# A selective-scan phase on one core: the position term by TensorE, the residual by TensorE and ScalarE, and paired input products

## The reference, cut to what matters

```python
x = x + L1_conv(ln_c(x), pos, W_in, conv_w, ...)      # ln_c: norm over the 64 channels of a pixel

xw = windows(x)                  # [b*nh*nw, 64, 8, 8]
xw = xw + pos                    # one position table for every window
seq = xw.reshape(b, 64, 64).transpose(0, 2, 1)        # 64 steps of 64 channels
x, z = split(seq @ W_in)         # 128 and 128 channels
x = silu(causal_conv(x, conv_w, 4 taps, by channel) + conv_b)
dt, B, C = split(x @ W_xproj)    # 4, 16, 16
dt = softplus(dt @ W_dt + b_dt)
h  = exp(dt * A) * h + (dt * x) * B      # 128 channels x 16 states, 64 steps, one after the other
y  = sum_n(h * C) + x * Dp
out = (y * silu(z)) @ W_out
```

## Time and profile before

| | |
|---|---|
| median of three runs | 8556.24 us |
| the profiled execution | 8588.41 us, span 8586.6 us |
| VectorE busy | 6791.2 us, 79% of the span |
| TensorE busy | 6282.9 us, 73% |
| GpSimd busy | 5185.6 us, 60% |
| ScalarE busy | 4293.2 us, 50% |
| DMA | 1253.45 MB, mean 146 GB/s |
| TensorE's granted clock, mean | 0.82 of full |

### The profile page before, as it was taken

The page is one execution under the profiler, slowest core; times in us unless marked ns, Lnnn a source line. Parts: engine busy times, 40 slices in busy tenths (PEclk is TensorE's granted clock), DMA queues, the critical chain, the costliest instruction groups (busy, mean ns, idle before and its releaser), DMA issues. The chain is left out here.

```text
span 8586.6 us, 102988 instructions
## 1 busy us (share of the span) xinstructions
PE 6282.9 (73%) x30668; PEld 2512.8 (29%) x30668; DVE 6791.2 (79%) x7924; ACT 4293.2 (50%) x5876; POOL 5185.6 (60%) x1723
## 2 busy tenths in 40 slices
PE   6888888888876777676776767777777777777455
PEld 3444444444431222222222222222222222222133
DVE  3555555555547999999999999999999999999634
ACT  1222222222225666666666666666666666666400
POOL 0000000000007999999999999999999999999500
PEclk8889889898977888888888888888888888888666
DMA  1111111111114655656556566565655656565553
GB/s 33 41 42 41 45 39 43 42 40 45 41 36 172 206 196 194 209 184 205 197 195 208 184 202 198 194 211 185 209 192 195 207 190 211 187 202 197 143 154 125
DMA packets 513971, 1253.45 MB, mean 146 GB/s; under 512 B 170085, under 2 KB 172297, under 8 KB 513673
## 3 DMA queue, kind: packets, MB, share of 16 engines
q1 hardware_dynamic: 513417, 1252.41, 45.2%
q0 software_dynamic: 512, 0.53, 0.0%
HBM read 943.30 MB, written 231.21 MB: 137 GB/s over the span
## 5 line engine op out<-in xcount | busy, mean ns | idle before, releaser
L1185 DVE TENSOR_TENSOR_SCAN b_h<-b_a,b_h 128x448 f32<-128x448 f32 x3584 | 3673.9, 1074 | 101.6 <-ACT b_a L1114 95.3
L1023 POOL TENSOR_TENSOR b_h<-b_h,b_ct 128x1792 f32<-128x1792 f32 x896 | 3571.1, 3989 | 279.6 <-DVE b_h L1185 265.8
L1114 ACT ACTIVATE b_a<-b_dts,decay 128x441 f32<-128x441 f32 x3584 | 2225.4, 629 | 1587.2 <-DVE b_h L1185 1560.3
L1035 POOL MEMSET b_seq<- 128x938 f32 x2 | 1.7, 880 | 2496.6 <-POOLq L798 2496.6
L1175 DVE TENSOR_TENSOR b_h<-b_dus,b_b 128x896 f32<-128x896 f32 x1344 | 1434.7, 1068 | 62.0 <-DMA b_dus<-d_dtu 60.6
L1282 PE MATMUL b_b<-b_rows,spread_b 16*128 16x512 f32 (+1 forms) x1792 | 567.6, 652 | 886.4 <-DVE b_h L1175 885.3
L1009 POOL TENSOR_TENSOR b_h<-b_dus,b_bt 128x896 f32<-128x896 f32 x448 | 933.9, 2085 | 44.8 <-DMA b_bt<-d_rows 28.1
L1290 PE MATMUL b_y<-b_h,fold 128*32 128x512 f32 (+1 forms) x7168 | 951.4, 658 | 8.1 <-POOL b_h L1023 8.1
L495 DVE TENSOR_TENSOR a_xg<-a_xd,a_pb 128x784 f32<-128x784 f32 x512 | 495.3, 967 | 519.4 <-PE a_pb L609 517.3
L1251 PE MATMUL b_w<-b_seq,w_conv 128*128 128x384 f32 (+1 forms) x896 | 557.4, 786 | 12.6 <-DMA b_seq<-b_seq 12.6
L1243 PE MATMUL b_w<-b_u,wx 128*64 128x512 f32 x448 | 361.1, 961 | 212.5 <-DVE b_dt L1207 212.5
(11 more groups left out here) (211 smaller groups left out, 8586.9 us busy)
## 6 DMA issues: line engine op xcount, KB each, us to landing
b_bt<-d_rows SPq DMA_DIRECT2D x448, 448.0 KB, 6.0
b_ct<-d_rows SPq DMA_DIRECT2D x448, 448.0 KB, 3.9
b_dts<-d_dt SPq DMA_DIRECT2D x448, 448.0 KB, 5.7
b_dus<-d_dtu SPq DMA_DIRECT2D x448, 448.0 KB, 6.2
a_xd<-a_xn SPq DMA_DIRECT2D x256, 196.0 KB, 3.4
d_dt<-b_dt SPq DMA_DIRECT2D x112, 448.0 KB, 2.5
d_dtu<-b_soft SPq DMA_DIRECT2D x112, 448.0 KB, 2.6
b_seq<-b_seq SPq DMA_DIRECT2D x112, 234.0 KB, 6.4
```

Source lines behind the costliest of these rows:

```text
L1023: nc.gpsimd.tensor_tensor(two, two, ct[t // 4 % 2][:].unsqueeze(1).broadcast_to([P, 2, TB]), ALU.mult).then_inc(hc_done, 2)
L1114: a(steps(bank(aa, k)), steps(half(dts[t % 4], k)), ACT.Exp, scale=decay[:, t % 4, t // 4:t // 4 + 1]).then_inc(a_done, 1)
L1185: v.tensor_tensor_scan(half(hh[t], k), bank(aa, k), half(hh[t], k), 0.0, ALU.mult, ALU.add).then_inc(h_done, 1)
```

## The change

- `residual` leaves VectorE. The output projection first adds the strip `xr` by an identity matmul, read in window order, and ScalarE copies the sum to `x3s` at t = 13 of unit 0.
- `sequences` is gone. GpSimd's norm writes its product in window order into one tile `seq_x`, and SP copies it four times: plain and shifted for each image. The position table is not added to the sequences. At the start TensorE makes two tables of it, 128 x 64 each, through the convolution and through z's projection; each later convolution and z adds its table by an identity matmul.
- VectorE's order becomes: scan t, then the input products named in `after`, some of them two tiles in one instruction. The step comes after scan 8.
- GpSimd does its input products in pairs (tiles 8 and 12 at t = 4, tiles 0 and 4 of the next unit at t = 13).
- ScalarE's work between the exponentials moves by one tile (norm end from 2 to 1, the rest from 4, 5, 6, 9, 11 to 5, 6, 7, 10, 12).
- SP loads bt 0, bt 1 and dus 0 before ct 3.

```diff
-                        def shift_seq(o):
-                            sp.wait_ge(seq_ready, 2 * o + 1)
+                        def shift_seq(c, normed):
+                            src = seq_x[:].rearrange("p w t -> p (w t)")
                             for i in range(2):
                                 flat = seq[i][:].rearrange("p w t -> p (w t)")
-                                sp.dma_start(flat[C * (1 - i):C * (1 - i) + C, 0:SL - 2],
-                                             flat[C * i:C * i + C, 2:SL]).then_inc(shifted, 16)
+                                q = slice(C * i, C * i + C)
+                                if i == 0:
+                                    sp.wait_ge(xn_ready, normed)
+                                elif c is not None:
+                                    sp.wait_ge(made, c + 2)
+                                sp.dma_start(flat[q, :], src[q, :]).then_inc(shifted, 16)
+                                sp.dma_start(flat[C * (1 - i):C * (1 - i) + C, 0:SL - 2], src[q, 2:SL]).then_inc(shifted, 16)
...
-                            sp.wait_ge(pb_done, row_no(i, 0, it))
+                            sp.wait_ge(pb_done, row_no(i, 1, it))
                             load_bt(2, i)
-                            sp.wait_ge(pb_done, row_no(i, 1, it))
...
+                                sp.wait_ge(pb_done, row_no(i, 3, it))
+                                sp.wait_ge(rows_stored[par], stored)
+                                load_bt(0, par)
+                                load_bt(1, par)
+                                sp.wait_ge(dtu_stored[par], stored)
+                                load_dus(0, par)
...
-                            nc.gpsimd.tensor_tensor(xc[:], xc[:], sq[:], ALU.mult).then_inc(xn_ready, 1)
+                            pool.wait_ge(shifted, 64 * (o - 1))
+                            nc.gpsimd.tensor_tensor(seq_x[:, :, CONV - 1:].rearrange("p w (r c) -> p r w c", c=WS), win(xc), win(sq),
...
-                            pool.wait_ge(bt_in[m % 2], it * 64 + (32 * i + 16 * (m // 2)))
-                            pool.wait_ge(folded, row_no(i, m, it) - 4)
-                            nc.gpsimd.tensor_tensor(hh[4 * m], dus[0][:], bt[m % 2][:], ALU.mult).then_inc(pb_done, 1)
+                            for b in range(2):
+                                pool.wait_ge(bt_in[b], it * 64 + (32 * i + 16 * (m // 2)))
+                            pool.wait_ge(folded, row_no(i, m + 1, it) - 4)
+                            nc.gpsimd.tensor_tensor(h_all[:, 4 * m:4 * m + 5:4, :], dus[:, 0:1, :].broadcast_to([P, 2, TB]), bt[:],
+                                                    ALU.mult).then_inc(pb_done, 2)
 
                         def unit(i, it, kind):
                             more = not (kind == LAST and i == 1)
                             for t in range(UNIT):
-                                if t in (3, 7):
-                                    inputs(i, 2 + t // 4, it)
-                                if t in (13, 15) and more:
-                                    inputs(1 - i, t // 15, it + i)
+                                if t == 4:
+                                    inputs(i, 2, it)
+                                if t == 13 and more:
+                                    inputs(1 - i, 0, it + i)
...
+                        def residual(c, q):
+
+                            act.wait_ge(made, c + 2)
+                            act.wait_ge(x3_stored, 16 * q)
+                            a(win(x3s), seqs(ww), ACT.Copy).then_inc(moved, 1)
...
-                                if t == 2 and norms:
+                                if t == 1 and norms:
...
-                                if t == 4:
+                                if t == 5:
...
-                                if t == 11 and more:
+                                if t == 12 and more:
                                     act.wait_ge(yz_ready, o - 1)
                                     move(spot(i, "z", it, kind), gate[1 - i][:])
+                                if t == 13 and i == 0 and kind != FIRST:
+                                    residual(spot(0, "out", it, kind), it - 1)
...
+                        def inputs(lo, hi, i, it):
+
+                            for t in range(lo, hi):
+                                if t < 4:
+                                    dve.wait_ge(dus_in[t], 16 * unit_no(i, it))
+                            if lo % 4 == 1:
+                                dve.wait_ge(bt_spread, row_no(i, lo // 4, it))
+                                dve.wait_ge(folded, row_no(i, lo // 4, it) - 4)
+                            v.tensor_tensor(h_all[:, lo:hi, :], dus[:, lo % 4:lo % 4 + hi - lo, :],
+                                            bb[:, 0:TB].unsqueeze(1).broadcast_to([P, hi - lo, TB]), ALU.mult).then_inc(b_done, hi - lo)
...
+                            after = {0: (1, 3), 1: (3, 4), 4: (5, 6), 5: (6, 8), 7: (9, 10), 9: (10, 11), 10: (11, 12),
+                                     12: (13, 14), 13: (14, 15), 14: (15, 16)}
                             for t in range(UNIT):
-                                if t % 4:
-                                    inputs(t, i, it)
-                                if not (kind == FIRST and i == 0 and t == 0):
-                                    scan_before(t, i, it)
+                                scan(t, i, it)
+                                if t in after:
+                                    inputs(*after[t], i, it)
                                 if t == 5 and not (kind == FIRST and i == 0):
                                     gated(1 - i, row_no(i, 0, it) - 1, unit_no(i, it) - 1)
-                                if t == 14 and i == 0 and kind != FIRST:
-                                    residual(spot(0, "out", it, kind), it - 1)
-                                if t == 7 and not (kind == LAST and i == 1):
+                                if t == 8 and not (kind == LAST and i == 1):
...
-                        def windows(c, src, weights, shifts):
+                        def windows(c, src, weights, shifts, at_pos):
 
                             pe.wait_ge(moved, c + 1)
                             for lo, hi in banks(TB):
                                 for n, (weight, shift) in enumerate(zip(weights, shifts)):
-                                    last = mm(ww[:, lo:hi], weight, src[:, lo // ST:hi // ST, shift:shift + ST],
-                                              start=(n == 0), stop=(n == len(weights) - 1))
+                                    mm(ww[:, lo:hi], weight, src[:, lo // ST:hi // ST, shift:shift + ST], start=(n == 0), stop=False)
+                                last = mm(ww[:, lo:hi], ident[:], at_pos[:].unsqueeze(1).broadcast_to([P, (hi - lo) // ST, ST]),
+                                          start=False, stop=True)
                             last.then_inc(made, 1)
 
                         def conv(c, i, o):
-                            pe.wait_ge(shifted, 32 * o)
-                            windows(c, seq[i], [w_conv[:, i, k, :] for k in range(CONV // 2)], range(CONV // 2))
+                            pe.wait_ge(shifted, 64 * o)
+                            windows(c, seq[i], [w_conv[:, i, k, :] for k in range(CONV // 2)], range(CONV // 2), pos_u)
 
                         def gate_in(c, i):
-                            windows(c, seq[i], [w_z[:, i, :]], [CONV - 1])
+                            windows(c, seq[i], [w_z[:, i, :]], [CONV - 1], pos_z)
...
-                        def out_proj(c, o):
+                        def out_proj(c, o, q):
 
                             pe.wait_ge(yz_ready, o)
+                            pe.wait_ge(xr_loaded, 16 * q)
                             pe.wait_ge(moved, c + 1)
+                            by_seq = xr[:].rearrange("p (r w c) -> p w r c", r=WS, c=WS)
                             for lo, hi in banks(TB):
+                                mm(ww[:, lo:hi], ident[:], by_seq[:, lo // ST:hi // ST], start=True, stop=False)
                                 for i in range(2):
-                                    last = mm(ww[C * i:C * i + C, lo:hi], w_out_t[:], yz[i][:, lo:hi], start=True, stop=True)
...
+                        pe.wait_ge(pos_ready, 2)
+                        for k in range(CONV // 2):
+                            mm(yy[:, 0:ST], w_conv[:, 0, k, :], seq_pos[:, k:k + ST], start=(k == 0), stop=(k == CONV // 2 - 1))
+                        mm(yy[:, ST:2 * ST], w_z[:, 0, :], seq_pos[:, CONV - 1:CONV - 1 + ST], start=True, stop=True).then_inc(pos_made, 1)
```

More of the change, by code:

```diff
@@ L773, in phase_b @@
                 dts = ring("dts", 4)
-                dus = ring("dus", 4)
-                bt = ring("bt", 2)
+                dus = sb("dus", [P, 4, TB])
+                bt = sb("bt", [P, 2, TB])
                 ct = ring("ct", 2)
@@ L1024, in unit @@
                                                             ALU.mult).then_inc(hc_done, 2)
```

(12 more changed lines are left out.)

92 lines of the change are left out of this document (30 added, 62 removed).

## The result

The changed kernel takes 8779.84 us (median of 4 runs, 8758.92 to 8782.95), against 8566.39 (4 runs) for the kernel before: ratio 1.0245, interval 1.0211 to 1.0279. It is 213 us slower. The forecast was 8594 us, the range ended at 8725. The profiled execution took 8782.95 us, its span is 8781.1. One execution each of experiments 11 and 12 was slow (13652.9 and 16226.3 us); the ratios leave them out, the medians keep them.

A forecast was written before the change was run, and what follows sets the result against it. VectorE was taken as the bound, with chains through ScalarE and TensorE behind it. 92.5 + 3.5 + .85 + .95 = 97.8 us a turn against 97.15, times 56, plus 2: +38 us, 8594 us; own range 8550 to 8640, eight in ten 8435 to 8725.

The forecast's parts named there:

- the gate's wait: VectorE's wait at the gate, now after scan 5 and a double input: 2.4 us a turn goes to about 0.
- VectorE's own work: VectorE's issue per turn: 91.8 less .98 (residual) and .2 (pairing), plus 1.9 for 16 waited-for products: 92.5 us.
- The setup's chain: Setup instructions that wait for each other: the next starts .03 us past the end, giving 1.10 us per waited-for product.
- The load of dus: dus 2 before the double input: 0 to 2.8 us late, given back at scan 2; nothing taken for the copies ahead.
- The rival that named this: dus lands behind the copies and scan 0's pair comes late, +1 us a turn each: 8705 us, chance .05.
- The norm's chain: From input 15 through TensorE and ScalarE into scan 2: wait 1.75 us a unit, 3.5 a turn.
- scan 14: VectorE waits there for ScalarE's residual copy, held up by the output projection: .95 us a turn.
- silu: ScalarE's silu block and tile 6's exponential end 5.8 us after scan 4, against VectorE's 5.98 us of work: no wait.
- softplus: ScalarE's exp and ln at tile 7, ahead of scan 8: wait .42 us a unit, .85 a turn.
- The rivals at 8432: TensorE stays at 2.4 GHz, the norm's centred product takes 1.77 for 3.20 us: 8432 us, chance .22.
- 8488 us (the own wait free): VectorE's wait behind its own instruction costs nothing, the turn is 95.9 us: 8488 us, chance .10.
- The one at 8715: TensorE slow in lengthened groups: projection 4.85 us, z .4 us more, residual and input 13 wait longer: 8715 us, chance .23.

The follow-up runs named there:

- experiments 11 and 12: 11: changed kernel, late copies, scan's product wait last, norm end at tile 2, residual copy at 14, no position part, 8483.7; 12: position kept, copy at 13, 8628.6 us.
- experiment 2: Changed kernel with each scan waiting first for ScalarE's exponential and last for its own input product: 8742.9 us, ratio 1.0191 to the kernel before.
- experiment 1: Changed kernel with the four sequence copies sent after the last load of dus: 8708.5 us, ratio 1.0151 to the kernel before.
- experiment 5: Kernel before with the residual's part alone (identity product, ScalarE's copy at tile 13, no residual on VectorE): 8593.7 us, ratio 1.0054.
- experiment 4: Changed kernel with the residual back on VectorE at t = 14, identity matmul and ScalarE's copy taken out: 8786.0 us, ratio 1.0239 to the kernel before.

## Why the prediction was wrong

The mechanism held: VectorE is the bound, the gate's wait is covered, and what was gained is eaten by chains. Two terms of the sum were too small. A third was too small as well, but the second hid it.

- **VectorE's own work.** The forecast turn has 92.5 us of issue. Measured: 100.97 less 7.1 of waits, 93.9. One failed step is "a waited-for product thus holds VectorE 1.10 us and not .98": it is 1.18. With the product's wait last it is 1.10 (experiment 2). The setup's chain does not show a scan with two waits. The count failed too, the other way: seven places a unit, not eight, and two of the 14 lie under longer waits. So 12 x .20 = 2.4 us stand in place of 1.9. That the sum's 16 was too many hides part of the miss. The other .9 us of the 1.4 the forecast did not have. At each wait VectorE also loses the overlap of two instructions, which no idle time counts. Scan 8 starts 1.38 us after input 9, which is .40 over .98, and .32 are counted; with six or seven waits a turn this is some .5 us, by estimate. The rest is not traced.
- **The load of dus.** The main failed step is "I take nothing for them; they cost up to 1 us a turn if dus 2 lands beyond 8 us". It lands 8.95 us after it is sent, in the mean, and VectorE stands 3.3 us a turn, where the forecast had 1.75 for that unit with the norm's chain in it. In the other unit the chain costs 1.8 us, as forecast. Net of what comes back, experiment 1 prices the copies' place at 1.3 us a turn, 71 us. I looked at landing times of single loads and not at how full the DMA engines are in that stretch. The rival that named this, with .05, had the mechanism but only +1 us for it, and its other half (the pair for scan 0) did not happen.
- **The norm's chain, hidden.** The spread ahead of the centred product of `x3s` was taken at 1.06 us and takes some 2. With the copies out of the way (experiment 1) this unit waits 2.7 us in place of 1.75, and of the .95 us between them .8 is the spread (1.89 us in the mean from its start to the centred product's) and .15 the centred product (3.35 against 3.20). Half of the chain's wait stands before scan 1, since the exponentials of tile 1 are queued behind the norm's first half; the forecast placed all of it at scan 2.
- **Right in place and near in size:** scan 14 .9 (forecast .95), with ScalarE waiting for the projection; scan 8 .6 (.85); z and projection at 2.4 GHz; the norm's product 2.09; GpSimd's pairs. The silu block costs .4 before scan 6, forecast 0.

Sum of the misses: 1.4 (own work) + 1.7 (dus and norm, 5.2 against 3.5) + .4 (silu) - .25 (softplus) - .1 (residual) = 3.15, all of the 3.2 us between 97.8 and 100.97. The base was a little off as well: the pair of turns that gave 97.15 us was short, the mean is 97.4.

By parts, from the ratios: the new order alone costs .48%, the residual part .54% alone (experiment 5), .91% on top of the order and nothing on top of order and position (experiment 4), the position part 1.91% on top of the order, 1.06% on top of both, 2.80% alone. These don't add up. That each part mostly moves the same chain at the strip's end would explain it, but no run shows it; a price holds only for the kernel that it was measured in. The Trainium skill's "VectorE: DVE Perf Modes" (The DRAIN you can't avoid) says of its own eight copies that a semaphore behind each costs nothing extra. That does not carry over to a scan that waits for its product: 1.18 and 1.10 us against .98. The same section adds that an instruction that is not held starts earlier, and the .98 us agrees.

The rivals at 8432 (TensorE at 2.4 GHz in the norm) and 8488 us (the own wait free) are out by the rows: the centred product takes 3.35 us, and the distance is 1.18. The first was a real possibility: in experiment 5 the same product ran at 2.4 GHz in every turn, 1.77 us, with TensorE idle for some .3 us before its spread, and in experiment 11 it took 1.87 in the mean. The one at 8715 came nearest in time for a wrong reason: input 13 waits only .06 us a turn for its spread, and the projection takes 3.8 us, not 4.85.

## What to carry to other kernels

Price a new transfer by how full the DMA engines are where it is sent, and by who is next in that queue; a share of .57 over the turn hid 1.0 in the stretch that counts. Put the wait that is met last at the end of the list: .08 us each here. Where an engine in order waits for a result with urgent work behind it, put that piece one tile later before anything is removed elsewhere: two such moves were worth 155 us here. Read the time of a short matmul group over many turns, not one: the spread that the forecast took at 1.06 us was a quick one of two kinds.

## What the hardware showed unexpectedly

- Two waits ahead of one VectorE instruction cost .08 us more when the one met last is handled first (1.18 against 1.10 us).
- The send of a load itself got longer on SP behind the four copies: dus 2 at 4067.29 took 1.61 us (1.55 in the mean, at most 2.13), where the other loads of dus take .52 to .60 in the mean. Behind the two copies of the kernel before it took 1.14 in the mean. With the copies sent later (experiment 1) no send of dus took more than .61.
- The spread of 16 rows took 2.05 us at a granted clock of .53 and 1.12 at 1.00, nearly twice the time for the same four matmuls.
- Idle time that ends with a DMA was labelled "issue" or with a fold that had long been done, for 168 us; moving only transfers took it away.
